# A Winograd-style convolution in sign arithmetic: its operand planes with columns outermost instead of rows

## The reference

```python
xn = xn * bn_gamma[None, :, None, None] + bn_beta[None, :, None, None]
t = jnp.where(xn >= 0.0, 1.0, 0.0)
t = jnp.where(xn <= 0.0, -1.0, t).astype(xn.dtype)
xc = jnp.clip(xn, -1.0, 1.0)
c_sum = jnp.sum(xc * t, axis=1, keepdims=True)
c_cnt = jnp.sum(jnp.abs(t), axis=1, keepdims=True)
y = _conv_nchw(t, conv_w, STRIDE, PAD) + conv_b[None, :, None, None]
b_sum = _conv_nchw(c_sum, ones_k, STRIDE, PAD) + beta_conv_b[0]
b_cnt = _conv_nchw(c_cnt, ones_k, STRIDE, PAD) + beta_conv_b[0]
return y * (b_sum / b_cnt)
```

## Time and profile before

| | |
|---|---|
| median of three timed runs | 922.51 us (922.1 to 922.61) |
| the profiled execution | 922.45 us |
| its span, first to last instruction | 920.7 us |
| first matmul of the convolution | 144.20 us |
| one image in the middle | 47.95 us (288 products and a small matmul pair) |
| busy in the span | PE 789.4, DVE 769.4, ACT 621.5, POOL 140.6 us |

### The profile page before, as it was taken

How to read it: one execution, slowest core, us unless ns; L and a number is a source line. 1 busy time by engine, 2 the same in 40 slices (tenths; PEclk the granted TensorE clock), 3 DMA queues, 4 the chain that set the end, 5 groups by cost and what they waited for, 6 DMA issues and landing times.

```text
span 920.7 us, 12815 instructions
## 1 busy us (share of the span) xinstructions
PE 789.4 (86%) x4722; PEld 468.2 (51%) x4722; DVE 769.4 (84%) x1193; ACT 621.5 (68%) x514; POOL 140.6 (15%) x158
## 2 busy tenths in 40 slices
PE   2100019999999999999999999999999999999996
PEld 1100015555555555555555555555555555555553
DVE  4899689999797979888888888797978787879756
ACT  2365738978685868677777777777778685858411
POOL 0089400011010111111111100111111111101011
PEclk9655559999999999999999999999999999999998
DMA  9999962489797979888788888796969696958578
GB/s 358 430 429 429 412 287 80 145 257 306 213 284 197 265 217 253 240 237 226 247 231 246 238 221 270 190 306 164 320 157 313 170 294 186 289 164 214 138 211 245
DMA packets 45446, 232.00 MB, mean 252 GB/s; under 512 B 11504, under 2 KB 12528, under 8 KB 41328
## 3 DMA queue, kind: packets, MB, share of 16 engines
q0 software_dynamic: 17856, 99.56, 41.9%
q1 hardware_dynamic: 26800, 132.05, 39.3%
q10 hardware_dynamic: 768, 0.12, 0.1%
HBM read 179.92 MB, written 51.79 MB: 252 GB/s over the span
## 4 chain that ended last, share of the span: by engine, by line
PE 79%; DVE 8%; DMA 5%; POOL 5%; ACT 2%; issue 1%; SPq 0%; DVEq 0%; ACTq 0%; POOLq 0%
PE acc L633 78%; DMA y<-x 3%; DVE st L762 2%; DMA xb<-x 2%; POOL V L328 1%; POOL U L345 1%; DVE st L775 1%; ACT U L414 1%; DVE y L1001 1%; DVE y L990 0%; POOL V L333 0%; POOL V L340 0%; POOL V L335 0%; DVE D L909 0%; POOL V L338 0%
## 5 line engine op out<-in xcount | busy, mean ns | idle before, releaser
L633 PE MATMUL acc<-V,U 128*128 128x385 f16 (+1 forms) x4608 | 768.2, 330 | 1.0 <-DVE y L990 0.6
L633 PEld LDWEIGHTS acc<-V,U 128*128 128x128 f16 x4608 | 450.5, 98 | 314.3 <-issue 1.9
L486 ACT ACTIVATE sn<-acc,inv_s 128x784 f32<-128x784 f32 x126 | 115.1, 914 | 193.2 <-PE acc L633 187.1
L355 POOL DMA_DIRECT2D y<-x x62 | 53.5, 862 | 710.5 <-DVE y L1001 697.0
L1001 DVE SCALAR_TENSOR_TENSOR y<-y,vec,bmap 128x1568 f32<-128x1568 f32 x63 | 115.6, 1834 | 0.1
L464 ACT ACTIVATE r<-xb,ab 128x1568 f32<-128x1568 f32 x64 | 106.6, 1690 | 5.5 <-ACT u L439 4.0
L439 ACT ACTIVATE u<-xb,ab 128x1624 f16<-128x1624 f32 x63 | 109.1, 1732 | 0.1
L449 ACT ACTIVATE T<-u 128x1680 f16<-128x1680 f16 x60 | 95.6, 1594 | 1.7 <-DVE D L909 1.7
L452 ACT ACTIVATE T<-T 128x1568 f16<-128x1568 f16 x58 | 87.6, 1510 | 1.8
L909 DVE TENSOR_TENSOR D<-T 128x1568 f16<-128x1568 f16 x62 | 60.4, 974 | 15.5 <-ACT T L452 15.3
L603 PE MATMUL csum<-mv,cst 128*128 128x32 f32 x2 | 0.6, 396 | 84.6 <-DVE mv L750 84.6
(11 more groups left out here) (127 smaller groups left out, 457.4 us busy)
## 6 DMA issues: line engine op xcount, KB each, us to landing
xb<-x SPq DMA_DIRECT2D x60, 812.0 KB, 6.3
y<-x POOLq DMA_DIRECT2D x62, 784.0 KB, 8.1
out<-y POOLq DMA_DIRECT2D x62, 784.0 KB, 9.8
y<-x SPq DMA_DIRECT2D x16, 1568.0 KB, 9.7
bmap<-map_rows SPq DMA_DIRECT2D x32, 784.0 KB, 6.0
xb<-x SPq DMA_DIRECT2D x14, 1568.0 KB, 10.8
V<-w_t SPq DMA_DIRECT2D x2, 1152.0 KB, 14.8
xb<-x SPq DMA_DIRECT2D x4, 420.0 KB, 9.2
```

The costliest lines, as they stand in the source:

```text
L486: nc.scalar.activation(sn[:, b, half], acc[:, b, :, 0:N], ACT.Copy, scale=inv_s[:, b:b + 1])\
L633: return nc.tensor.matmul(by_row(acc[:, g % 2, bank, 0:N])[:, :, lo:hi], U[:, ci, digits, k, dx, co * P:(co + 1) * P], by_row(V[:, a, ci, ...
```

## The change

From image 1 on a plane's element is `w * 7 + q`: the column is outside and the quadruple inside. Image 0 keeps the old order on all engines.

- **TensorE**: all products of images 1 to 15 read and write one contiguous run, of 392 or 385 numbers. `image(1, 1)` and `image(NI - 2, 0)` are now written out and the loop runs six times instead of seven, since image 1 also holds THIRD of image 0's last group in the old order.
- **ScalarE**: `planes` reads `u` in the new order by a hand-built pattern (six row taps, then 56 columns, then seven quadruples that lie 4 rows = 448 bytes apart) and writes 6 x 392 = 2352 numbers instead of 30 rows = 1680. `snapshot` reads `acc` with a step of 7 numbers (28 bytes) and writes `sn` in row order.
- **VectorE**: the six operations of `transform` work on contiguous runs of 392, as many numbers as before. `ends` reads `acc` with a step of 7. Image 0 has functions of its own with the old code.

```diff
+        taps = T[:, :, :].rearrange("p r w -> p (r w)")[:, 0:8 * N].rearrange("p (k f) -> p k f", f=N)
+        taps8 = T8[:, :, :].rearrange("p r w -> p (r w)").rearrange("p (k f) -> p k f", f=N)
+        diff = D[:, :, :, :].rearrange("p j r w -> p j (r w)").rearrange("p j (k f) -> p j k f", f=N)
...
+        def row_order(n, t):
+            if isinstance(n, int) and n == 0:
+                return by_row(t)
+            return t.rearrange("p (w q) -> p q w", q=Q)
+        def row_taps(g):
+            base = u[:, g % 2, g // 2:g // 2 + HR + 2]
+            return bass.AP(base.tensor, base.offset, [list(base.ap[0]), [W, K6], [1, W], [4 * W, Q]])
...
             def planes(m, g):
-                nc.scalar.activation(T[:, 30:60], u[:, g % 2, h:h + HR + 2], ACT.Relu, scale=2.0).then_inc(t_ready, 1)
+                nc.scalar.activation(taps[:, 2:8].rearrange("p k (w q) -> p k w q", q=Q), row_taps(g), ACT.Relu,
+                                     scale=2.0).then_inc(t_ready, 1)
                 if not vector_t8(m, g):
                     act.wait_ge(t_ready, s + 1)
-                    nc.scalar.activation(T8[:, :], T[:, 30:30 + HR], ACT.Copy, scale=4.0, bias=-3.0)\
+                    nc.scalar.activation(taps8, taps[:, 2:6], ACT.Copy, scale=4.0, bias=-3.0).then_inc(t8_ready, 1)
...
             def snapshot(n, g, half):
-                nc.scalar.activation(sn[:, b, half], acc[:, b, :, 0:N], ACT.Copy, scale=inv_s[:, b:b + 1])\
+                sums, kept = acc[:, b, :, 0:N], sn[:, b, half]
+                if not (isinstance(n, int) and n == 0):
+                    sums = sums.rearrange("p k (w q) -> p k q w", q=Q)
+                    kept = kept.rearrange("p k (q w) -> p k q w", w=W)
+                nc.scalar.activation(kept, sums, ACT.Copy, scale=inv_s[:, b:b + 1]).then_inc((snap1, snap2)[half], 1)
...
+                    into = acc[:, g % 2, bank, Q * lo:Q * hi]
+                    plane = V[:, a, ci, VPLANE[k], h, Q * (lo + dx - 1):Q * (hi + dx - 1)]
                 return nc.tensor.matmul(
-                    by_row(acc[:, g % 2, bank, 0:N])[:, :, lo:hi],
-                    U[:, ci, digits, k, dx, co * P:(co + 1) * P],
-                    by_row(V[:, a, ci, VPLANE[k], h])[:, :, lo + dx - 1:hi + dx - 1],
+                    into, U[:, ci, digits, k, dx, co * P:(co + 1) * P], plane,
...
-            with pe.Fori(0, (NI - 2) // 2) as i:
-                image(2 * i + 1, 1)
+            image(1, 1)
+            with pe.Fori(0, (NI - 4) // 2) as i:
                 image(2 * i + 2, 0)
+                image(2 * i + 3, 1)
+            image(NI - 2, 0)
             image(NI - 1, 1, final=True)
...
+            def transform(m, a, g):
+                nc.vector.tensor_scalar(taps[:, 0:2], taps[:, 3:6:2], 2.0, None, ALU.mult).then_inc(t4_ready, 1)
+                nc.vector.tensor_tensor(diff[:, 1, 1:3], taps[:, 1:7:5], taps[:, 0:5:4], ALU.subtract)\
+                  .then_inc(aq_done, 1)
+                nc.vector.tensor_tensor(diff[:, 0], taps[:, 4:8], taps8, ALU.subtract).then_inc(cq_done, 1)
+                nc.vector.tensor_tensor(V[:, a, c, 2:5:2, h], diff[:, :, 2], diff[:, :, 1], ALU.add)
+                nc.vector.tensor_tensor(V[:, a, c, 3:6:2, h], diff[:, :, 2], diff[:, :, 1], ALU.subtract)
+                nc.vector.tensor_tensor(V[:, a, c, 0:2, h], diff[:, 0, 2:4], diff[:, 0, 0:2], ALU.subtract)\
...
             def ends(n, g):
-                        out=quads(y[:, g])[:, :, 3 * k], in0=by_row(acc[:, b, k, 0:N]), scalar=scale[:, b:b + 1],
+                        out=quads(y[:, g])[:, :, 3 * k], in0=row_order(n, acc[:, b, k, 0:N]), scalar=scale[:, b:b + 1],
```

More of the change, by code:

```diff
@@ L443, in planes @@
             def planes(m, g):
-                s, h = 4 * m + g, g // 2
+                s = 4 * m + g
                 act.wait_ge(cq_done, s)
@@ L578, in _ @@
                         act.wait_ge(part_done, 1)
-                    nc.scalar.activation(sn[:, 1, half, bank], acc[:, 1, bank, 0:N], ACT.Copy, scale=inv_s[:, 1:2])\
+                    nc.scalar.activation(by_row(sn[:, 1, half, bank]), row_order(NI - 1, acc[:, 1, bank, 0:N]),
+                                         ACT.Copy, scale=inv_s[:, 1:2])\
                       .then_inc(snap if bank else part_snap, 1)
@@ new lines, in first_other_planes, with first_transform @@
+            def first_other_planes(g, d):
+                nc.vector.tensor_tensor(v_planes(0, g, 3, 2), d[:, :, 2:HR:4], d[:, :, 1:HR:4], ALU.subtract)
+                nc.vector.tensor_tensor(v_planes(0, g, 0, 1), rows(d[:, 0], 2), rows(d[:, 0], 0), ALU.subtract)\
+                  .then_inc(v_ready, 1)
+            def first_transform(g):
+                at_least(dve, v_ready, g)
+                first_differences(g, D)
+                dve.wait_ge(cq_done, g + 1)
+                dve.wait_ge(aq_done, g + 1)
+                nc.vector.tensor_tensor(v_planes(0, g, 2, 2), D[:, :, 2:HR:4], D[:, :, 1:HR:4], ALU.add)
+                first_other_planes(g, D)
@@ L923, in transform @@
-            def transform(m, a, g):
-                at_least(dve, v_ready, 4 * m + g)
-                differences(m, g, D)
-                if not (isinstance(m, int) and m <= 1):
-                    dve.wait_ge(third_done, 4 * m - 6 + 2 * (g // 2))
-                first_planes(m, a, g, D)
-                other_planes(m, a, g, D)
+                nc.vector.tensor_tensor(diff[:, 0], taps[:, 4:8], taps8, ALU.subtract).then_inc(cq_done, 1)
+                if not (isinstance(m, int) and m <= 1):
+                    dve.wait_ge(third_done, 4 * m - 6 + 2 * h)
@@ L1057, in _ @@
             first_group(1, T01, D)
-            other_planes(0, 0, 0, D00)
-            other_planes(0, 0, 1, D)
-            transform(0, 0, 2)
+            first_other_planes(0, D00)
+            first_other_planes(1, D)
+            first_transform(2)
             pair_sum(0, 0)
-            transform(0, 0, 3)
+            first_transform(3)
             mid(0, 0)
```

48 lines of the change are left out of this document (26 added, 22 removed).

## The result

The changed kernel takes 967.08 us (median of 4 runs, 966.59 to 968.19) beside 922.32 us for the kernel before (4 runs on the same chip): a ratio of 1.0487, with a 95% interval of 1.0469 to 1.0505. It is 4.9% slower where I had forecast 0.6% faster. The profiled execution took 967.42 us, its span 965.6.

A forecast was written before the change was run, and what follows sets the result against it. PE was taken as the bound, at 47.95 us an image. The profiled 922.45 us less 5.7 for the products, other terms costing nothing, gave 916.8 us; own range 914.5 to 918.5 (68 in 100), full range 914.0 to 922.6.

The forecast's parts named there:

- PE's gain: Products of 385 columns as one run take 163.75 ns instead of 165.83, 2.08 ns less each; -5.7 us in all.
- The 914.3 us that stand beside my sum: Time if a product of 385 columns took 162.9 ns by the Trainium skill's issue-gap rule, which the forecast did not follow.
- The first rival: Products on PE cost what they cost now, 166 ns, so the time stays at 922.5 us; 12 in 100.
- The step in PSUM's reads: Snapshots and `ends` reading PSUM with a step: taken as free; if doubled, +0.65 us per snapshot, +0.41 per `ends` operation.
- Y: What a snapshot on ACT costs more by its stepped PSUM read; 2Y = 1.3 us if doubled.
- The step in SBUF's reads: ACT's `planes` reading numbers 448 bytes apart: taken as free; if doubled, +1.96 us per `planes`.
- X: What `planes` on ACT costs more by its stepped SBUF read; 1.96 us if doubled.
- The condition of the rival: ACT becomes the bound: PE stands still once X + 2Y is over 2.3 us, needing both reads doubled (3.3); 8 in 100.
- The room of 2.9 us: How late the second snapshot around `planes` on ACT may be before PE waits; 2.3 left after the change.
- The cover of `ends`: DVE's second `ends` has 2.1 us left before the next FIRST is due, 1.3 with the doubled read.
- The rival's time: With ACT as the bound at 51.1 us an image over 14 images, 967 us; 8 in 100.
- What I had said would show it: Image at 47.55 us, `planes` about 2.15 (4.1 if doubled); wrong if PE's waits name a snapshot; DVE's longer wait costs nothing.

The follow-up runs named there:

- that execution: Profiled run of the changed kernel with DVE's `mid` and `ends` put ahead of `transform`: 967.44 us, ratio 1.0503.
- that kernel: The changed kernel with `mid` alone put ahead of `transform` on DVE, `ends` staying behind it: 956.24 us, ratio 1.0369.
- the last kernel: The changed kernel with T8 moved from ACT to DVE and `mid` put ahead of `transform`: 928.4 us, ratio 1.0067.
- two kernels with the same sum of waits: The changed kernel with `mid` and `ends` ahead of `transform`, 967.44 us, and with `mid` alone ahead, 956.24 us.

## Why the prediction was wrong, point by point

- **PE's gain**: right in size, 2.08 ns for each product of 385 columns forecast and measured, though both ends of it were read 0.2 ns too low: 165.83 to 163.75 forecast, 166.04 to 163.96 measured. The split by columns that I started from, 400 and 398 cycles, isn't in the rows (166.26 and 166.04 ns, 399.0 and 398.5 cycles). The products of 392 gained 0.41 ns more, for which I had no term, about 0.6 us in all. (The 914.3 us that stand beside my sum come to 914.5 by the same count of products.) The kernels without the step in `planes` took 916.54 and 915.98 us, forecast 916.8. The first rival is out.
- **The step in PSUM's reads**: right, Y = 0 (904 and 619 ns).
- **The step in SBUF's reads, the term that failed.** I wrote "I take the step as free", from DVE's `crow`. X was 4.29 - 2.15 = 2.1 us, which is the doubled read that I had as its other end. The price was in the range of costs, but not its effect in the range of times.
- **The condition of the rival, the second failure.** I wrote that PE stands still once X + 2Y is over 2.3 us, and that a doubled SBUF read alone doesn't reach it. It came to 2.1, and PE stood still 3.3 us an image. The room of 2.9 us was right for one snapshot on its own, but lateness adds up from quarter to quarter where ACT's work of a quarter (12.31 and 13.90 us) is over PE's 11.86. The stretch in the earlier trace rows showed it: from 549.88 to 561.84 us, one quarter, ACT had only 0.44 us idle and can't take 0.56 + 2.1 us more.
- **The cover of `ends`, the third.** I had 2.1 us of room for `ends` and a later T "from idle time that it has". With the real X, T comes 0.56 + 2.1 = 2.7 us later, `ends` stand behind it in DVE's queue, and 2.7 - 2.1 = 0.6 us of wait would follow. The three waits for `ends` of an image measured 0.71, 0.22 and 0.80 us, and the one that belongs to the group of the earlier trace rows is the 0.22: the mechanism is shown, but the 0.6 gives its size only roughly.
- **The rival's time**: 967 us against 967.08 is a coincidence. It was worked out for ACT as a full bound at 51.1 us an image with both reads doubled; ACT has 45.8, and what fills the 50.8 us are waits in two queues.
- **What I had said would show it**: `planes` at 4.1 us for doubled reads, and a waits' row of PE that names a snapshot. Both came. DVE's wait for T did grow to over 50 us (63.6), and it didn't "cost nothing".
- **The chance**: the Trainium skill's rule on lines and DVE's row spoke against each other, and the row was of another engine and another type. It could bear a price for DVE's fp32 reads and little for ACT's fp16; 8 in 100 was too low.

## What to carry to other kernels

A stepped read is priced on the engine and with the type that will do it; where no row shows that, the doubled price belongs in the range of the time, not only in that of the cost. A longer operation is followed along every queue behind it: the waits of another engine's instructions for it hold what stands behind them, and lateness has to be summed over all groups whose work is over the bound's pace. If a layout must be turned around, let the reordering engine touch pairs of 2-byte numbers, or do it where fp32 numbers are read from PSUM; both cost next to nothing here.

## What the runs showed of the hardware that I had not expected

- ACT, fp16 in SBUF, 2352 numbers: reads in runs 2153 ns, 8 bytes apart 2594, 14 bytes and more 4042 to 4588; pairs 2258. Writes of singles 4 bytes apart 2839 ns, 8 apart 5463, 16 and more apart about 10100 to 11000; pairs 2345.
- DVE, two fp16 inputs, 784 results: 559 to 567 ns in runs, 1524 to 1543 with reads 448 bytes apart, 3244 to 3427 with writes 14 bytes apart.
- PSUM, fp32, read 28 bytes apart: free for ACT (904 ns against 914) and for DVE (619 against 619).
- A matmul over seven runs of 55 columns costs 166.04 ns in this stream, over one run of 385 163.96: the breaks cost 2.1 ns of it.
- After one wait of PE of about 2 us the granted clock fell to the half level for 3.4 us in some images and not in others (mean 0.82 after the wait at 544.78, 1.00 at 648.30), six times in that execution. With waits of 1.54 us in their place it never did; the one fall of that kernel came in the start stretch after a wait of 2.34 us, and the same wait of 2.34 us at 175.29 in the last kernel brought none. Five falls fewer were worth 8.3 us between two kernels with the same sum of waits.
